# Next block's h normalised from raw tokens and turned by VectorE and HBM in place of TensorE

## The reference

```python
xn = layernorm(x)                                  # (4, 1024, 256)
# s: attention network of xn
h = rmsnorm(xn, attn_norm_w)                       # times a weight per feature
q, k, v = h @ Wq, h @ Wk, h @ Wv                   # 8 heads of 128
# linear attention in chunks of 128 tokens, per head, S starts at 0
attn = where(causal, q_c @ k_c.T, 0)
o = attn @ v_c + q_c @ S;  S = S + k_c.T @ v_c
x2 = xn + (rmsnorm(o, out_norm_w) over heads) @ Wo
h2 = rmsnorm(x2, mlp_norm_w)
s = x2 + (silu(h2 @ Wgate) * (h2 @ Wup)) @ Wdown
# g: gated network of xn, both operands of each product rounded to FP4 in groups of 16
g = silu(fp4(silu(fp4(xn) @ fp4(w_gate).T) * (fp4(xn) @ fp4(w_up).T)) @ fp4(w_down).T)
out = x + s * g
```

## Time and profile before

| | us |
|---|---|
| median of 3 runs | 1059.18 |
| lowest and highest | 1056.58, 1059.53 |
| the profiled execution | 1058.67 |
| its span, from the first to the last instruction | 1056.9 |
| TensorE busy in the span | 1049.1 |
| VectorE busy | 878.0 |
| ScalarE busy | 559.3 |
| GpSimd busy | 47.2 |

### The profile page before, as it was taken

The page is one execution under the profiler, slowest core; times in us unless marked ns, Lnnn a source line. Parts: engine busy times, 40 slices in busy tenths (PEclk is TensorE's granted clock), DMA queues, the critical chain, the costliest instruction groups (busy, mean ns, idle before and its releaser), DMA issues.

```text
span 1056.9 us, 18900 instructions
## 1 busy us (share of the span) xinstructions
PE 1049.1 (99%) x6790; PEld 960.0 (91%) x6790; DVE 878.0 (83%) x1779; ACT 559.3 (53%) x1604; POOL 47.2 (4%) x68
## 2 busy tenths in 40 slices
PE   9999999999999999999999999999999999999998
PEld 6899999999999989999999989999999999999997
DVE  6778888787887888888777898889888888888887
ACT  6765766756757657657666634343333333333332
POOL 1000000000000000000000000101010010101010
PEclk9999999999999999999999999999999999999999
DMA  6555355455464563654546522253423333423213
GB/s 219 163 173 171 108 173 169 140 159 165 141 187 130 171 181 109 187 171 150 164 131 196 162 90 76 80 160 100 132 74 120 91 114 100 121 85 102 79 59 111
DMA packets 166238, 143.10 MB, mean 135 GB/s; under 512 B 28800, under 2 KB 162944, under 8 KB 166144
## 3 DMA queue, kind: packets, MB, share of 16 engines
q1 hardware_dynamic: 165456, 141.88, 43.5%
q10 hardware_dynamic: 688, 0.00, 0.0%
HBM read 77.27 MB, written 64.57 MB: 134 GB/s over the span
## 4 chain that ended last, share of the span: by engine, by line
PE 91%; DMA 3%; DVE 2%; SPq 1%; issue 1%; ACT 1%; POOL 0%; ACTq 0%; DVEq 0%; POOLq 0%
PE ps L263 71%; PE ps L726 5%; PE ps L778 5%; PE ps L772 4%; PE ps L756 4%; DMA moved<-work 2%; DMA r_gate<-moved 1%; SPq L417 1%; PE ps L861 1%; PE ps L654 1%; PE ps L614 1%; SPq L498 1%; DVE work L1521 0%; ACT work L949 0%; DVE work L1404 0%
## 5 line engine op out<-in xcount | busy, mean ns | idle before, releaser
L263 PE MATMUL ps<-r_k,r_gate_up 128*128 128x512 f32 x768 | 185.2, 391 | 0.0
L263 PEld LDWEIGHTS ps<-r_k,r_gate_up 128*128 128x128 f32 x768 | 141.5, 188 | 27.2 <-DVE work L1652 0.4
L263 PE MATMUL ps<-r_o,onT 128*128 128x256 f32 x768 | 106.9, 288 | 0.0
L263 PE MATMUL ps<-r_h,r_k 128*128 128x512 f32 (+1 forms) x393 | 105.2, 403 | 0.0
L263 PEld LDWEIGHTS ps<-r_q,r_v 128*128 128x128 f32 x768 | 99.7, 191 | 5.0 <-DVE r_v L1656 0.3
L263 PE MATMUL ps<-r_q,r_v 128*128 128x256 f32 x768 | 102.3, 283 | 0.0
L969 ACT ACTIVATE work<-ps 128x128 f32<-128x128 f32 x256 | 67.1, 278 | 59.6 <-PE ps L778 59.4
L263 PE MATMUL ps<-r_h,r_q 128*128 128x512 f32 x384 | 98.2, 391 | 0.0
L263 PE MATMUL ps<-r_v,r_h 128*128 128x512 f32 x384 | 97.4, 390 | 0.0
L263 PEld LDWEIGHTS ps<-r_o,onT 128*128 128x128 f32 x768 | 95.8, 190 | 0.2
L1165 ACT ACTIVATE r_v<-work 128x512 fp32r<-128x512 f32 x64 | 40.5, 633 | 99.6 <-DVE work L1652 99.5
(11 more groups left out here) (159 smaller groups left out, 2034.5 us busy)
## 6 DMA issues: line engine op xcount, KB each, us to landing
moved<-work SPq DMA_DIRECT2D x63, 512.0 KB, 2.9
r_gate<-moved SPq DMA_DIRECT2D x252, 128.0 KB, 2.5
kept_h<-work SPq DMA_DIRECT2D x31, 384.0 KB, 2.6
work<-kept_h SPq DMA_DIRECT2D x124, 96.0 KB, 2.2
work<-in_L_attn_hidden_states SPq DMA_DIRECT2D x15, 512.0 KB, 5.1
kept<-work SPq DMA_DIRECT2D x9, 514.0 KB, 4.6
kept_h<-work SPq DMA_DIRECT2D x9, 512.0 KB, 3.6
kept_xq<-work SPq DMA_DIRECT2D x8, 512.0 KB, 5.7
```

What stands on the lines that cost most here:

```text
L263: done = pe.matmul(out_ap, a, b, start=first and n == 0, stop=last and n == 2, skip_group_check=skip)
```

## The change

- ScalarE makes h from the raw tokens at once: h = x_in * a + b, where a is the product of both norms' factors and b is -mean * a (`h_factors`, on VectorE in step 1). It does so at the end of step 1.
- VectorE turns its 32x32 squares in step 2, back into x_in (`turn_blocks`, two instructions). SyncE stores it to a new HBM tensor `kept_h` in step 3, behind the write of the exchange, and loads it into h_flat behind the exchange's four reads.
- ScalarE, in step 4, multiplies h_flat by the norm weight in place and then copies it to HI, for each of the two halves of the features; VectorE subtracts for LO in the late part of step 4.
- TensorE's eight transposes in step 3 go. Its wait for hT moves from ahead of step 4's scores to the end of step 4, and so do that step's values; ScalarE copies them behind the squares of o.
- fp4_max moves from early in step 4 to late in step 3, and the transpose of the weight piece from early in step 4 to behind the low halves.

All of it happens in blocks 0 to 6, for the next block. The diff, cut to its core:

```diff
@@ SyncE
-                def exchange(value, o=None, turned_o=None, again=True):
+                def exchange(value, o=None, turned_o=None, again=True, next_h=None):
...
                     sp.dma_start(moved.rearrange("b p x -> p b x"), leaving.rearrange("p b i x -> p b (i x)"))\
                       .then_inc(moved_out, 16)
+                    if next_h is not None:
+                        sp.wait_ge(h_turned, KD + next_h)
+                        sp.dma_start(kept_h[next_h % HALVES].rearrange("a p x -> p a x"),
+                                     in_quads(x_in.rearrange("p c d -> p (c d)"))).then_inc(h_stored, 16)
...
                         sp.dma_start(arriving[q * QUAD:(q + 1) * QUAD].rearrange("p a i x -> p a (i x)"),
                                      moved[q].rearrange("(a p) x -> p a x", a=QUADS)).then_inc(moved_in, 16)
+                    if next_h is not None:
+                        sp.wait_ge(h_stored, 16 * next_h)
+                        load_turned(h_flat, kept_h[next_h % HALVES], h_loaded)
...
+                                 next_h=n + 1 if h == CH - 1 and n + 1 < BLOCKS else None)
@@ TensorE
-                    if h == CH and ahead:
-                        pe.wait_ge(hT_ready, (n0 + s) * KD + 2 * KD)
                     for c in range(CH):
                         done = pe.matmul(ps[:, B_SCORE, c * P:(c + 1) * P], kT[:, c * P:(c + 1) * P],
...
-                    if ahead or h < CH:
+                    if (ahead or h < CH) and h != CH:
                         values(*((1, h, s) if h < CH else (0, h - CH, 1 - s)))
...
-                    if h == CH - 1 and ahead:
-                        pe.wait_ge(h_ready, n0 + s + 1)
-                        pe.wait_ge(k_perm_ready, t0 + j + 2)
-                        pe.wait_ge(k_ready, t0 + j + 2)
-                        turn_h(0)
-                        pe.wait_ge(attn_ready, t0 + j + 1)
-                        turn_h(1)
...
                         out_projection((j - LAG) % H, t0 + j - 1)
+                    if h == CH and ahead:
+                        pe.wait_ge(hT_ready, (n0 + s) * KD + 2 * KD)
+                        values(0, 0, 1 - s)
@@ ScalarE
-                def normed_h(parity, value):
-
-                    act.wait_ge(xn_ready, value)
-                    act.wait_ge(gu_ready, value)
+                def normed_h(n):
+
+                    act.wait_ge(h_factor_ready, n)
+                    act.wait_ge(gu_ready, n + 1)
                     for c in range(CH):
-                        done = act.activation(h_sb[:, c, :], xn[:, parity, c, :], ACT.Copy, scale=small[:, HR, c:c + 1])
+                        done = act.activation(h_sb[:, c, :], x_in[:, c, :], ACT.Identity, bias=small[:, HB, c:c + 1],
+                                              scale=small[:, HG, c:c + 1])
...
+                def turned_hi(parity, n):
+                    act.wait_ge(h_loaded, 16 * QUADS * n)
+                    for k in range(KD):
+                        act.activation(landed(h_flat, k), landed(h_flat, k), ACT.Copy, scale=nw_attn[:, k:k + 1])\
+                           .then_inc(h_scaled, 1)
+                        act.wait_ge(h_scaled, (n - 1) * KD + k + 1)
+                        act.activation(as_tokens(hT[:, parity, HI, k, :]), landed(h_flat, k), ACT.Copy).then_inc(hT_hi, 1)
...
-                    if h == CH - 1 and ahead:
-                        turned_hi(0, 1 - s, (n0 + s) * KD + KD + 1)
-                        turned_hi(1, 1 - s, (n0 + s) * KD + KD + 2)
+                    if h == CH and ahead:
+                        turned_hi(1 - s, n0 + s + 1)
                     if h == CH and n0 + s in (1, 2):
                         weights4_hi(n0 + s - 1, h_flat[:, 0:N4])
...
                     o_root(t0 + j + 1)
+                    if h == CH and ahead:
+                        copy_v(t0 + j + CH + 1, 0, 0)
...
-                    if h == 2 and ahead:
-                        normed_h(1 - s, n0 + s + 2)
+                    if h == 1 and ahead:
+                        normed_h(n0 + s + 1)
@@ VectorE
+                def h_factors(parity, mine):
+
+                    settled(dve.tensor_tensor(small[:, HG, :], small[:, HR, :], ln_factor[:, parity, 0, :], ALU.mult), mine)
+                    dve.scalar_tensor_tensor(small[:, HB, :], mv[:, parity, :, 0], -1.0, small[:, HG, :],
+                                             ALU.mult, ALU.mult).then_inc(h_factor_ready, 1)
...
+                def turned_lo(parity, n):
+                    for k in range(KD):
+                        dve.wait_ge(hT_hi, n * KD + k + 1)
+                        dve.tensor_tensor(as_tokens(hT[:, parity, LO, k, :]), landed(h_flat, k),
+                                          as_tokens(hT[:, parity, HI, k, :]).bitcast(F32), ALU.subtract)\
+                           .then_inc(hT_ready, 1)
...
-                    if h == CH and rounds_piece:
-                        dve.transpose(h_flat[:, 0:PIECE4[n - 1]].rearrange("p (b t) -> p b t", t=QUAD),
-                                      piece.rearrange("p (b t) -> p b t", t=QUAD)).then_inc(piece_ready, 1)
-                    if h == (0 if final else CH):
+                    if h == 0 and final:
                         fp4_max(x_of_block, x_scale, mine)
...
+                    if h == CH - 1 and not final:
+                        fp4_max(x_of_block, x_scale, mine)
+                    if h == CH and ahead:
+                        turned_lo(1 - s, n + 1)
+                    if h == CH and rounds_piece:
+                        dve.wait_ge(hT_ready, (n + 2) * KD)
+                        dve.transpose(h_flat[:, 0:PIECE4[n - 1]].rearrange("p (b t) -> p b t", t=QUAD),
+                                      piece.rearrange("p (b t) -> p b t", t=QUAD)).then_inc(piece_ready, 1)
...
                     if h == 2 and ahead:
                         normalize(1 - s)
-                    if h == CH - 1 and ahead:
-                        turned_lo(0, 1 - s, n * KD + KD + 1)
-                        turned_lo(1, 1 - s, n * KD + KD + 2)
+                        dve.wait_ge(xn_ready, n + 2)
+                        dve.wait_ge(h_ready, n + 1)
+                        turn_blocks(x_in.rearrange("p c d -> p (c d)"), h_flat, h_turned)
```

45 lines of the change are left out of this document (22 added, 23 removed).

## The result

The changed kernel takes **1067.58 us** in the median of 4 runs (1067.09 to 1069.47), the kernel before 1058.79 in 4 (the 3 of the table and one more). The ratio is 1.0089, 95% interval 1.0077 to 1.0101: 8.8 us slower, where 2.5 were forecast. The profiled execution took 1067.99 us around a span of 1066.3, so the two spans differ by 9.4 us. The granted clock is 0.997 or more in every profile here; it plays no part.

The account below looks back on a forecast made before the run. TensorE, busy 1049.1 of 1056.9 us, was taken to bound the kernel. Terms -6.1 + 0.6 + 3.25 + 4.7 = +2.45 us took the profiled 1058.67 to 1061.2 us, "no change" on its slow side; range 1053.5 to 1067.5 us.

Parts of the forecast that it names:

- The transposes, -6.1: Step 3, blocks 0 to 6: dropping 56 TensorE transposes returns 0.87 us per block, 6.1 us, not 273 ns each.
- Steps 1 and 2, +0.6 and 0: Factors delay step 1's state updates: 0.3 us in block 0, 0.1 in blocks 2, 4, 6; step 2's extra work hidden.
- Step 4, +3.25: TensorE waits for the new hT: 0.35 us in odd blocks, 0.55 in even. T is the start of a step's scores.
- Blocks 1 and 2, +4.7: Step 5: late weight piece delays ScalarE, VectorE's root and state updates; 2.45 us lost in block 1, 2.25 in block 2.
- The rival that the pieces don't matter: Blocks 1 and 2: the late root is caught up before L778, 4.7 us fall away, 1056.5 us; chance 0.17.
- The store in the way: Rival: the store of h delays step 3's exchange 1.9 us; TensorE waits 0.9 us more per block, 1067.5 us; chance 0.24.
- Block 7, 0: Last block: no loss counted in the sum, 0 us.

Follow-up runs that it names:

- experiment 8: The kernel before, with each of its 56 TensorE transposes executed twice; 1064.59 us against 1058.83, ratio 1.0057.
- experiment 6: Changed kernel with the weight piece rounded behind the root and, in even blocks, ScalarE's first-state copy ahead of the values' copy; 1061.80 us against 1058.83, ratio 1.0030.
- experiment 9: Experiment 5's kernel with the first state copied ahead of the values and the two factors behind VectorE's state updates; 1056.86 us against 1058.34, ratio 0.9987.
- experiment 11: Experiment 5's kernel with the next tokens' norm leaving out the mean, so ScalarE adds no bias; one run, 1057.43 us.
- experiment 1: Changed kernel with ScalarE rounding the weight piece behind the root in blocks 1 and 2; 1063.61 us against the kernel before's 1059.07, ratio 1.0048.
- experiment 2: Changed kernel without scaling in place: ScalarE scales and copies in one operation, VectorE subtracts in eight quarters; 1066.94 us, ratio 1.0072 to the kernel before.
- experiment 3: Changed kernel without scaling in place and with the weight piece rounded behind the root; 1062.38 us, ratio 1.0032 to the kernel before.
- experiment 4: Changed kernel without the store of h to HBM and its four loads; 1067.20 us, ratio 1.0068 to the kernel before.
- experiment 7: Changed kernel with the piece behind the root and, in the last block, the store of x2 behind the exchange; 1064.41 us against 1058.83, ratio 1.0055.
- experiment 5: Changed kernel with the piece behind the root and the norm weight folded into the projection weights at the start; 1058.56 us against 1058.83, ratio 0.9999.
- experiment 10: The kernel before with only step 4's values moved behind the output projection, their copy behind the root; 1063.66 us against 1058.34, ratio 1.0046.
- experiment 12: Experiment 10's kernel with VectorE's piece transpose and group maximum behind the state updates, the piece rounded behind the root; 1059.15 us against 1058.71, ratio 1.0004.

## Why the prediction was wrong

Between the two profiles lie 9.4 us, where the sum gave 2.45. The missing 7 us are 1.7 of the transposes' return, 1.6 in steps 1 and 2, 2.8 in step 4 and 1.9 in block 7, less 0.3 in step 5 and 0.7 elsewhere. So the mechanisms that the prediction named were there. The steps that failed are "hidden" for steps 1 to 3, a chain sized too short in step 4, and a block put at nothing without a reason.

**The transposes, -6.1: the price was right, the return was not.** Experiment 8 has 0.87 us in each of blocks 1 to 6. The 275 ns that the Trainium skill gives a 128x128 transpose, of bf16 ("TensorE: Matmul & The Clock Gate", PE-mode transpose), agree with the duration of 273 for these in float32. Taken as the price of each they would have made it 15.4 us; the runs decide for the pitch. But leaving them out returned 0.87 to 0.79 us in odd blocks, 0.67 in blocks 2, 4 and 6, and nothing in block 0, 4.4 in all. The sentence "The scores' mask is then done some 2.3 us into step 3, and L772 needs it at 5.7: hidden" followed the mask and not what VectorE and ScalarE do behind it. In blocks 2, 4 and 6 that is the first state, whose copy (L997) comes last on ScalarE; experiment 6 gave 0.2 us of it back in blocks 2 and 4. In block 0, 1.0 us of the missing 1.7, it is the turned keys as well: VectorE's root comes 2.37 us into step 3 in place of 1.82, behind the 1.30 us of the two new transposes, the keys behind the root, and L758 waits. That is read from the trace and not taken away by a run; with the first state's copy ahead (experiments 6 and 9) block 0 still gains nothing.

**Steps 1 and 2, +0.6 and 0: measured +1.4 and +0.8.** Step 1 lost 0.28 us in block 0, as the 0.3 forecast, and 0.2 in blocks 2, 4 and 6 in place of 0.1. There the factors lose time only together with the late copy of the first state: with that copy moved alone (experiment 6), step 1 is at its old length. The same copy makes the 0.2 us of step 2. "The norm makes ScalarE's copies about 1 us late, as it did in step 3 before: hidden too" failed: the norm takes 0.37 us longer than the 1.70 of L927, and either without these 0.37 us (experiment 11) or with the first state's copy ahead of the values' (experiment 6) step 2 is back. In step 3 before, the transposes' 0.87 us on TensorE covered such a delay; that is argued from the order, not tested. In block 6, step 1 is 1.08 us longer, most of it VectorE's wait of 0.80 us for arrivals. With the same orders there it is 0.2 in experiments 1 to 3, but 0.83 and 0.74 in experiments 4 and 7: luck of the execution, as are the 0.40 that block 5 gained.

The Trainium skill has the price of the bias ("ScalarE: Activation LUTs", What ACT_TABLE_LOAD costs): each per-partition operand of an activation adds about 93 ns. The trace agrees, with 595 against 504 ns in experiment 11 and 0.71 to 0.73 against 0.63 us for the scaling in place against the copy. An estimate by it ahead of the run would have priced the norm at 2.07 us and each scaling at 0.72.

**Step 4, +3.25: measured +6.0.** The mechanism was as forecast to the order of the instructions; experiment 5 took it away and got 5.4 us back. What was off are sizes. In odd blocks (1 and 5) the loss was 0.55 us, not 0.35. The scalings took 0.72 in place of 0.63, so the chain ended at T+7.90, not 7.7, but TensorE went on at T+7.96, close to the 7.9 forecast; the larger part is that the values behind the wait took 1.49 us and not 1.37. In even blocks it was 0.8 to 1.0 us, not 0.55: the chain starts 0.42 us later there (T+4.94 against T+4.51), and 0.2 were allowed. In block 3 it was 1.33, where VectorE waited 0.95 us for arrivals, and 0.93 of the 1.33 are there without the transfers of h too (experiment 4). The prediction also took it for granted that moving the values costs nothing. Experiments 10 and 12 show that this holds in the changed kernel's order of VectorE and not in the old one; it is no part of the miss.

**Blocks 1 and 2, +4.7: right in the mechanism, with luck in the number.** 4.45 us were measured, and experiment 1 took 3.3 of them away by cutting the chain that was described. The rival that the pieces don't matter falls with it. But block 1 lost 2.77 us in place of 2.45 and block 2 lost 1.68 in place of 2.25, and the two errors cancel in part. The prediction's own working for block 1, updates ending 9.5 us into the step against 7.2, gives 2.3 and not 2.45. The 1.1 us that block 1 keeps in experiment 1 come with a root at 1.6 us, which the prediction had held to be harmless; in blocks 3 to 6 of the changed kernel, with the root at 1.58 to 1.67 us, it was.

**The store in the way: wrong.** It gave 1067.5 us, the time that was measured, for a reason that experiment 4 refutes: the exchange landed in 3.0 to 3.1 us with the store behind it, and step 4 is as long without the store. What the Trainium skill says of rings ("DMA: Bandwidth & Descriptors", Queues, rings and completion order), that descriptors are consumed in order, fits these landings. A time that comes out right is no evidence for its rival.

**Block 7, 0: measured +1.9, and open.** The prediction put it at nothing, since nothing of the change stands in it, and didn't ask what the transfers there would meet. In the nine other profiles of kernels built on the changed one it is +0.6 to +5.1 (the last in experiment 2, whose profiled execution was 2.7 us over its median); in three built on the kernel before 0.1 to 0.2. In three of the four profiles with the old path of the next tokens VectorE waits 0.8 us in step 4 for arrivals, which leaves the stores of that step 0.6 us more ahead of the next exchange; in none of the changed ones, nor in experiment 8, which lost only 0.2 all the same. That the distance to the stores delays the exchange fits most of these profiles, but not experiments 5 and 11, where it was issued 3.3 and 3.0 us behind them and still took 3.4 and 3.7 us. Experiment 7 shows that moving one store doesn't pay. Why the arrivals of step 4 come late in the one family and not in the other isn't settled.

The sum by the runs: the transposes -4.4, steps 1 and 2 +2.2, step 4 +6.0, step 5 +4.4, block 7 +1.9, the rest -0.7; 9.4 us between the profiles.

## What to carry to other kernels

When work is taken off the engine that sets the pace, what it hid becomes visible: before counting the gain, list for each step what comes just in time on the others, and follow it to its last consumer, not to the first. An operation that is moved later uncovers what now comes sooner on its own engine (here the state products, 1.37 us), and an order that looks like a cost of the change may be what makes the move possible. A fix to one link of a chain of two engines can end in a wait that only changes its owner, as in experiment 3: price the other link first.

## What the runs showed of the hardware

- An activation of 128x256 from SBUF took 595 ns with a per-partition scale and bias and 504 with the scale alone (91 ns); one of 128x512 took 710 to 730 with a per-partition scale and 630 without.
- Eight three-operand subtractions of 128x128 took 2.18 us (273 ns from one to the next) where two of 128x512 with two operands took 1.28 to 1.38.
- A 128x128 float32 transpose on TensorE lasted 273 ns, and eight in a row cost its path 0.87 us, 109 ns each.
- A 512 KB exchange with a 512 KB store 0.4 us behind it landed in 3.0 to 3.1 us, and in 2.9 to 3.0 without the store; the reading back that followed landed up to 0.9 us later (block 5).
- The same exchange, issued 2.3 us behind the last of two stores (1 MB), landed in 3.6 (experiment 8) to 4.8 us; 2.9 to 3.0 us behind in 2.9 to 3.0 in three profiles and 3.7 in experiment 11; 3.3 us behind in 3.4 (experiment 5), and 1.5 to 1.6 us behind in 4.0 (experiments 6 and 9).
